# A decoder layer in one block for all engines, with orders of work of their own for the two kinds of attention slot

## What is computed

```python
x = x + attn(layernorm(x))                 # 16 heads of 16, with biases
x = x + xattn(layernorm(x), ctx, mask)     # keys and values from ctx; a masked score is 1e-9
h = gelu(layernorm(x) @ ternary(W_fc).T)   # 256 -> 1024, exact gelu
x = x + (layernorm(h) * ln_w + ln_b) @ ternary(W_proj).T
# attn: softmax(Q K.T / 4) V, then an output projection
# ternary(W): sign(W) * min(round(|W| / (mean|W| + 1e-6)), 1)
```

## Time and profile before

| | us |
|---|---|
| median of 3 runs (2600.8 to 2608.62) | 2607.31 |
| profiled execution, its own time | 2609.64 |
| its span, first to last instruction | 2607.8 |

### The profile page before, as it was taken

How to read it: one execution, slowest core, us unless ns; L and a number is a source line. 1 busy time by engine, 2 the same in 40 slices (tenths; PEclk the granted TensorE clock), 3 DMA queues, 4 the chain that set the end, 5 groups by cost and what they waited for, 6 DMA issues and landing times. The chain is left out here.

```text
span 2607.8 us, 72523 instructions
## 1 busy us (share of the span) xinstructions
PE 2210.0 (85%) x29047; PEld 1457.0 (56%) x29047; DVE 2033.7 (78%) x4023; ACT 1609.8 (62%) x2352; POOL 1026.5 (39%) x719
## 2 busy tenths in 40 slices
PE   3367888888889888888988888888865799999999
PEld 3134555555555555555555555555533477777777
DVE  5257888888888888888888888888753588888887
ACT  2245666666666666666666666665532687788776
POOL 0133443433443433344443344343221454555553
PEclk8679999999999999999999999999987899999999
DMA  3356786666677676667767666776431333333332
GB/s 86 67 88 111 125 131 119 121 127 120 123 124 125 121 119 126 118 123 129 123 122 127 118 122 124 122 126 117 82 68 36 67 83 94 97 89 81 95 97 58
DMA packets 450752, 276.75 MB, mean 106 GB/s; under 512 B 299344, under 2 KB 401104, under 8 KB 450512
## 3 DMA queue, kind: packets, MB, share of 16 engines
q1 hardware_dynamic: 447728, 270.68, 55.7%
q10 hardware_dynamic: 2784, 2.43, 0.3%
HBM read 54.87 MB, written 33.55 MB: 34 GB/s over the span
## 5 line engine op out<-in xcount | busy, mean ns | idle before, releaser
L616 ACT ACTIVATE prob<-exp_bank 128x1024 f32<-128x1024 f32 x512 | 523.0, 1022 | 289.2 <-PE exp_bank L870 285.6
L714 DVE TENSOR_REDUCE cross_mx<-score_bank 128x8 f32<-128x1024 f32 x256 | 311.0, 1215 | 136.2 <-PE score_bank L852 136.2
L714 DVE TENSOR_REDUCE self_mx<-score_bank 128x8 f32<-128x1024 f32 x256 | 310.4, 1213 | 135.1 <-PE score_bank L852 135.1
L550 POOL TENSOR_TENSOR xs<-xn,xs 128x1024 f16<-128x1024 f32 x64 | 136.1, 2127 | 686.6 <-ACT xs L643 686.6
L1267 PE MATMUL hbk<-wfcT,ffn_xhl 128*128 128x512 f16 x1024 | 265.5, 383 | 28.5 <-DMA ffn_xhl<-ffn_xs 26.6
L550 POOL TENSOR_TENSOR ahl<-attT,ahl 128x512 f16<-128x512 f32 x128 | 148.0, 1156 | 349.6 <-ACT ahl L621 349.6
L1227 DVE SCALAR_TENSOR_TENSOR ghl<-tbk,lnwc,ghl 128x512 f16<-128x512 f32 x256 | 187.9, 735 | 100.3 <-ACT ghl L1158 100.3
L1243 PE MATMUL ybk<-wpT,ghl 128*128 128x256 f16 x2048 | 260.5, 273 | 0.8 <-DVE ffn_y L1212 0.7
L1243 PEld LDWEIGHTS ybk<-wpT,ghl 128*128 128x128 f16 x2048 | 197.9, 98 | 66.0 <-DVE ghl L1227 0.9
L1158 ACT ACTIVATE ghl<-tbk,lnwc 128x512 f16<-128x512 f32 x256 | 174.0, 680 | 68.3 <-PE tbk L1257 68.3
L746 DVE STREAM_TRANSPOSE out_bank<-out_bank 128x512 f32<-128x512 f32 x256 | 183.9, 718 | 40.3 <-PE out_bank L887 40.3
(11 more groups left out here) (162 smaller groups left out, 4654.9 us busy)
## 6 DMA issues: line engine op xcount, KB each, us to landing
self_stk<-self_qk SPq DMA_DIRECT2D x768, 64.0 KB, 2.4
cross_stk<-cross_qk SPq DMA_DIRECT2D x768, 64.0 KB, 2.4
self_src<-in_x SPq DMA_DIRECT2D x32, 512.0 KB, 5.7
ctx_in<-in_ctx SPq DMA_DIRECT2D x32, 512.0 KB, 6.3
x_scratch<-xn SPq DMA_DIRECT2D x32, 512.0 KB, 5.5
ffn_src<-x_scratch SPq DMA_DIRECT2D x32, 512.0 KB, 3.8
out<-ffn_y SPq DMA_DIRECT2D x32, 512.0 KB, 3.6
self_stk<-self_negmT SPq DMA_DIRECT2D x64, 128.0 KB, 3.8
```

What stands on the lines that cost most here:

```text
L550: nc.gpsimd.tensor_tensor(out, src, hi, ALU.subtract).then_inc(lo_ready, 1)
L616: act.activation(prob[:, p % 3], ebank[:, :, :], ACT.Exp, scale=EXP_SCALE).then_inc(b.exp_done, 1)
L714: dve.tensor_reduce(a.mx[:, 8 * m:8 * m + 8].rearrange("p (j r) -> p r j", r=2), sbank[:, :, :].rearrange("p r (j k) -> p r j k", j=4), AX ...
```

## The change

One block holds all parts. `setup`, `attention` and `ffn` now hand out pieces (`prep`, `att`, `mlp`), and each engine's program strings them together. Each of the five slot orders is written twice, for cross slots (`if s.a.cross`) and for self slots. The loop over attention groups is gone on ACT, DVE and POOL. The maxima DMAs are issued by ACT (`maxima_rows`), not by SP. The FFN's step -1 (load and norm of group 0) stands before the last two attention slots on SP, POOL, ACT and DVE; ACT waits for all stores of x2 only before the first write of `ghl`.

```diff
 def decoder_layer_kernel(nc, ins, out):
...
+        LAST = 2 * (NG + 4)
+        @block.sync
+            att.load_first(sp)
+            prep.load_weights(sp)
+            att.slots(lambda s: att.sync(sp, s), 0, 3)
...
+            att.slots(lambda s: att.sync(sp, s), 8, LAST)
+            mlp.load_first(sp)
+            mlp.sync(sp, -1)
+            att.slots(lambda s: att.sync(sp, s), LAST, LAST + 2)
+            mlp.unrolled(sp, lambda i: mlp.sync(sp, i))
+        @block.gpsimd
+            prep.constants(pool)
+            att.slots(lambda s: att.gpsimd(pool, s), 0, 2)
+            att.slots(lambda s: att.gpsimd(pool, s, prep.bo_done), 2, 3)
+            att.slots(lambda s: att.gpsimd(pool, s), 3, LAST)
+            mlp.gpsimd(-1)
...
+        @block.scalar
+            prep.load_small(act)
+            att.slots(att.scalar, 0, 3)
+            prep.weights_high(act)
+            att.slots(att.scalar, 3, 4)
+            prep.magnitudes(act)
+            att.slots(att.scalar, 4, 6)
+            prep.projection_out(act)
+            att.slots(att.scalar, 6, LAST)
+            mlp.scalar(-1)
+            att.slots(att.scalar, LAST, LAST + 2)
+            mlp.steps(act, mlp.scalar)
+        @block.vector
+            att.slots(att.vector, 0, 2)
+            att.prime_queries(dve, 0, prep.consts)
+            prep.mask_parts(dve)
+            att.prime_queries(dve, 1, prep.consts)
+            prep.weights_low(dve)
+            att.slots(att.vector, 2, 4)
+            att.prime_values(dve)
+            prep.ternary(dve)
+            prep.tables(dve)
+            att.slots(att.vector, 4, 6)
+            prep.ternary_out(dve)
+            prep.tables_out(dve)
+            att.prime_cross(dve)
+            att.slots(att.vector, 6, LAST)
+            mlp.vector(-1)
+            att.slots(att.vector, LAST, LAST + 2)
+            mlp.steps(dve, mlp.vector)
+        @block.tensor
+            prep.turn_weights(pe)
+            att.slots(att.tensor, 0, 4)
+            prep.mask_products(pe)
+            att.slots(att.tensor, 4, 6)
+            prep.turn_ternary(pe, att.maxima_out, att.exp_done)
+            prep.table_products(pe)
+            prep.await_tables(pe)
+            att.slots(att.tensor, 6, LAST + 2)
+            mlp.steps(pe, mlp.tensor)
```

`prime_cross` fills the constant rows of both `cross_stk` buffers (before at L1029) and of the cross values. `turn_ternary` waits for the self exponentials and maxima of group 0, since it uses their PSUM banks; the fresh tables need one set of eight f32 products (128x256) where two sets of eight stood. SP's and POOL's orders and ACT's new piece:

```diff
-            turn_context()
-            stacks(0)
-            stacks(1)
-            turn_input()
-            stacks(2)
-            maxima()
-            store()
-            load()
+            if s.a.cross:
+                turn_context()
+                load()
+                stacks(0)
+                stacks(1)
+                turn_input()
+                stacks(2)
+                store()
+            else:
+                stacks(0)
+                stacks(1)
+                turn_input()
+                stacks(2)
+                load()
...
-            residual()
-            biased()
-            low_outputs(b, s.gb, 0)
+            if s.a.cross:
...
+                low_outputs(b, s.gb, 0)
+                residual()
+                biased()
+            else:
...
+                residual()
+                low_outputs(b, s.gb, 0)
+                biased()
...
+            def maxima_rows():
+                if s.ga is not None:
+                    act.wait_ge(a.mT_out, s.ga + 1)
+                    for r in range(2):
+                        act.dma_start(a.stk[HALF * r + STACK:HALF * (r + 1), s.ra, 0].rearrange("p j k t -> p (j k) t"),
+                                      a.negmT[:, :].unsqueeze(1).broadcast_to([H, FT // 2 * KT, T])).then_inc(a.m_in, 16)
```

More of the change, by code:

```diff
@@ L1040, in ffn @@
-def ffn(nc, program, sh, x2_dram, out):
+            if s.a.cross:
+                tile(0)
+                tile(1)
+                scores(0)
+                shifted(0)
+                tile(2)
+                scores(1)
+                shifted(1)
+                tile(3)
+                shifted(2)
+                scores(2)
+                weighted(0)
+                shifted(3)
+                scores(3)
+                weighted(1)
+                shifted(4)
+                scores(4)
+                products(0, 1)
+                shifted(5)
+                scores(5)
+                products(2, 3)
+                weighted(2)
+                scores(6)
+                shifted(6)
+                values(0, 1)
+                scores(7)
+                shifted(7)
+                values(2, 3)
+                turn_maxima()
+                masked_values()
+                weighted(3)
+            else:
+                tile(0)
+                tile(1)
+                scores(0)
+                shifted(0)
+                tile(2)
+                scores(1)
+                shifted(1)
+                tile(3)
+                scores(2)
+                shifted(2)
+                weighted(0)
+                scores(3)
+                shifted(3)
+                scores(4)
+                products(0, 1)
+                shifted(4)
+                scores(5)
+                weighted(1)
+                shifted(5)
+                scores(6)
+                products(2, 3)
+                shifted(6)
+                scores(7)
+                weighted(2)
+                shifted(7)
+                values(0, 1)
+                turn_maxima()
+                weighted(3)
+                values(2, 3)
@@ L1046, in ffn @@
+        part.stored, part.maxima_out, part.exp_done = stored, slf.mT_out, slf.exp_done
+        return part
+def ffn(nc, program, sh, x2_dram, out, before):
     x2_groups = x2_dram.rearrange("(n b) s d -> n s b d", b=G)
@@ L1092, in steps @@
         def steps(engine, body):
[L1094 to L1095 removed]
+            body(0)
             with engine.Fori(1, NG // 2 - 2) as i:
```

712 lines of the change are left out of this document (379 added, 333 removed).

## The result

The changed kernel takes **2675.25 us** (median of 4 runs, 2667.86 to 2681.86) against 2604.36 us of the kernel before beside it (4 runs): ratio 1.0275, 95% interval 1.0238 to 1.0312. It is slower by 2.7%, where the prediction said 2538.8 us and faster. The profiled execution took 2681.76 us, with a span of 2680.0 us.

What follows compares the result with a forecast made beforehand. It took attention to be bound by the issue time of SP's queue. Start -51, preparation +9, steady part -11 and end -15.5 sum to -68.5 us, from 2607.3 to 2538.8 us; range 2485 to 2583.

Steps and rivals of the forecast that it cites:

- What bounds the kernel: Steady attention: the issue time of SP's queue binds, some 22 us a slot from cast to scores; PE and DVE have slack.
- The start: Before attention: x load issued first, so the first self product starts at 23.5 instead of 74.81 us; -51 us (-47 to -56).
- the preparation: FFN weights' preparation, moved into the filling slots, mainly between slots 5 and 6: +9 us (4 to 15).
- The end: Attention to FFN: the FFN's first load and norm move before the last two slots; -15.5 us (-8 to -20).
- the 1.28 for Gelu's table: At the FFN's start: Gelu's table load becomes exposed, taking 1.28 us off the end's gain.
- No loops: Steady part: ACT, DVE and POOL written out must fetch more instructions; +0.3 us a pair of slots.
- the term for the maxima DMAs: Every attention slot: moving the two maxima DMAs from SP's to ACT's queue costs or gains 0.
- the term for the stretch from scores(0) to the cast of tile(3): PE's new order in cross and self slots shortens this stretch: -0.7 us a pair (-2 to +2).
- the steady term: Steady attention: (-0.7 + 0.3) us a pair over 28 pairs, -11 us (-56 to +50).
- D: Rival: maxima from ACT's queue land late, shifted(0) holds PE and SP's chain; slower, 2634 us at 1.5 us a slot; 4%.
- A: Rival: PE was the bound; the orders close half its idle time, the pair falls to 52.5 us, total 2455 us; 8%.

Runs made afterwards that it cites:

- e1: Kernel after, with the slot orders of the kernel before and the maxima's DMAs back on SP: 2553.61 us, ratio 0.9823.
- e5: Kernel before, with the maxima's DMAs issued by ACT instead of SP, and ACT, DVE and POOL written out without loops: 2662.65 us, ratio 1.0245.
- e4: Kernel after, plus ten scratch products on PE ahead of its wait for the stack of scores(0): 2607.35 us, ratio 1.0032.
- e3: Kernel after, with the maxima's DMAs issued by SP again, behind block 2's stack DMAs: 2767.27 us, ratio 1.0654.
- e8: Kernel after, with the maxima's DMAs issued by POOL at the end of its slot instead of ACT: 2859.55 us, ratio 1.1011.
- e6: e1 with tile(2) and tile(3) moved ahead of scores(0) on PE, ACT and DVE: 2606.83 us, ratio 1.0028.
- e12: Kernel after, with tile(2) ahead of scores(0) and tile(3) one place earlier, in cross slots only: 2557.75 us, ratio 0.9820.
- e9: e1 with tile(2) ahead of scores(0), tile(3) right behind it, and shifted(0) and shifted(1) later: 2696.35 us, ratio 1.0369.

## Why the prediction was wrong

Step by step, by its own terms:

- **What bounds the kernel** was right. SP's chain closes in the kernel after as before, 60.2 us a pair by its six parts.
- **The start** was right in its first half (23.5 predicted, 24.17 measured), and the preparation was mis-sized: 17.7 us and not 9, beyond the bound of 15. The self half's first maxima are 48.0 us earlier, those of group 1 only 36.7, so 11.3 of the 17.7 arise between these two, around slots 5 and 6, where the +9 had been put: both stack copies (100.31, 4.50 us) stand on DVE ahead of the maximum for which PE waits 6.87 us. No row read here says where the rest goes.
- **The end** was right to 0.1 us, partly by luck. Attention ends 8.2 us later behind its landmark where 7 was forecast, and the 1.28 for Gelu's table is not seen (FFN to end +0.4). The wait that sets the 8.2 is PE's for DVE's `ue` (2074.34, 10.37 us), not the one for ACT from which the 7 was worked out.
- **No loops**: +0.3 a pair was predicted. e1 has it all and its pair is 56.1 against 56.4, so the cost is nil. The page counts 205 fetches on one queue as before and 69 smaller ones (35 before) on another. The rule of the Trainium skill that the prediction cited (Runtime: NRT & Kernel Launch, Instruction fetch mechanics), that sequential fetching is mostly hidden, agrees with this run.
- **The step that failed first** is the term for the maxima DMAs, put at 0 because they stood behind the 24 stacks, so "they are not in the chain", and because ACT has room. It asked whether ACT had time to issue them, and who waited behind them on ACT. It did not ask what their transfers meet. They now fall into SP's block 2, whose eight issues are on the chain, and stretch them by 1.2 us a slot and the landing by 0.2. e5 shows that this alone costs 2.5%. The Trainium skill (Perfetto Trace Analysis, DMA Optimizations) says that balancing DMAs across the engines that can issue them may help where issuing is the bottleneck. e5 is a case where it did not, with a ratio of 1.0245: the two DMAs that moved, of 26 a slot that fill the stack, were not on the chain, and now disturb those that are.
- **The second step that failed** is the term for the stretch from scores(0) to the cast of tile(3), -0.7 a pair with bounds -2 and +2. With the clock held it was right in sign: e4 gives 10.9 against 12.0, a gain of 1.1. But every duration in that sum came from rows at the full clock. The prediction had noted PE's slack of 7 us a pair and hid work in it, without asking where the slack collects. It collects ahead of scores(0), as a pause of 3.1 us on average, after which tile(2), on the chain, mostly ran at the half clock. That costs 13.3 - 10.9 = 2.4 a pair. The order did not make this pause alone: e5 has it at 1.6 us with the old orders. No run has the new orders with early maxima and unstretched issues, so how the 2.4 splits between the two is open.
- So the steady term is made of +2.4 (block 2), +0.4 (landing), +2.4 (clock), -1.1 (the segment with the clock held) and some -0.3 for the rest: +3.8 or 3.9 a pair, 31 pairs, 120 us.
- **The rivals.** D had the sign, with 4%, and named the right neighbourhood, the maxima's new queue, but the wrong victim: PE's wait at shifted(0) is 1.3 us in all. In e3 and e8, where the maxima are late, its mechanism is there and costs 3 us a slot and more. A doesn't hold either: e6 frees PE of SP's chain, and its round is no shorter, with PE 86% busy between 300 and 1800 us and the rest waits of the order, for DVE above all. The range ended at 2583 and did not hold 2675, because the bound of +2 a pair on the order left out that the clock could fall, and the maxima's move had no bound at all. It was also narrower than its own terms: +2 for the order and +0.9 for the fetches over 28 pairs are +81 for the steady part, not +50, and the sum with that would be 2631.

## What to carry to other kernels

When a DMA is moved to another engine's queue, ask not only who waits for it and what waits behind it, but which transfers of the critical queue it will now run beside. When an in-order engine gets slack, find where the slack collects: for TensorE one long pause ahead of a product on the critical chain cost 2.4 us a pair here that the short pauses of before did not, and moving one useful tile into that pause (e12) is better than filling it with nothing (e4). An order of work that interleaves two chains should be changed a step at a time, with the sum over a slot read from both: e6 and e9 opened SP's chain and lengthened the round of PE and DVE.

## What the runs showed of the hardware

Two 128 KB transfers that ACT issues lengthen the issue itself of SP's 64 KB DMAs beside them, 886 ns against 685 on average in after and 849 against 666 in e5, not only their landing (3.5 against 2.6 us in after). What the two queues share there is not settled by these runs. The granted clock, after pauses of 2.55 and 3.69 us, gave the half level for the next tile (2.59 and 2.40 us); after 1.96 us before and 1.07 and 1.43 us in e12 and e4 the tile took 1.47. These rows are no threshold: in the trace of after a tile behind a pause of 2.10 us was slow, and one behind 2.69 us was not.
